# VectorE's instructions moved between slots in a fused linear-attention and feed-forward kernel

## The reference

```
q, k, v = xn Wq', xn Wk', xn Wv'           (512 -> 128 each)
r_t     = q_t M_t',  M_{t+1} = 0.99 M_t + v_t' k_t / 4    (a scan over the 2048 steps)
s       = (r Wo') * sigmoid(gate)           (128 -> 512)
h       = layernorm(xn) * gamma + beta
y       = silu(h W1 + b1)                   (512 -> 2048)
z       = y W2 + b2                         (2048 -> 512)
g       = silu(xn + 0.5 z)
out     = x + s * g
```

## Time and profile before

| | |
|---|---|
| three runs | 1338.12, 1339.03, 1340.52 us; median 1339.03 |
| the profiled execution | 1339.37 us; its span 1337.6 us, mean granted clock 0.977 |
| busy, share of the span | TensorE 92%, VectorE 84%, ScalarE 80%, GpSimd 29% |
| chunk 0 (from 51.7 us) | 97.0 us |
| chunks 1 to 14, each | 77.6 us |
| chunk 15 and the tail slots | 73.5 us and some 28.7 us |

### The profile page before, as it was taken

How to read it: one execution, slowest core, us unless ns; L and a number is a source line. 1 busy time by engine, 2 the same in 40 slices (tenths; PEclk the granted TensorE clock), 3 DMA queues, 4 the chain that set the end, 5 groups by cost and what they waited for, 6 DMA issues and landing times.

```text
span 1337.6 us, 19050 instructions
## 1 busy us (share of the span) xinstructions
PE 1225.3 (92%) x6144; PEld 633.7 (47%) x6144; DVE 1121.2 (84%) x1894; ACT 1075.0 (80%) x1885; POOL 382.0 (29%) x465
## 2 busy tenths in 40 slices
PE   1279999999999999999999999999999999999994
PEld 0034454545545454554545455454545545454551
DVE  5978798888979888897988889798888979888774
ACT  1349888888888888888888888888888888888885
POOL 4115241321414132141413214141422314142111
PEclk8579999999999999999999999999999999999998
DMA  9201021120302112030211203021120303011011
GB/s 327 54 2 32 1 57 40 32 64 2 93 1 64 32 33 64 5 91 0 65 31 33 64 12 84 1 75 21 33 63 15 82 1 82 14 36 29 18 46 32
DMA packets 38837, 61.21 MB, mean 46 GB/s; under 512 B 9553, under 2 KB 9809, under 8 KB 38737
## 3 DMA queue, kind: packets, MB, share of 16 engines
q1 hardware_dynamic: 38448, 59.87, 17.4%
q10 hardware_dynamic: 288, 0.08, 0.0%
HBM read 43.14 MB, written 16.78 MB: 45 GB/s over the span
## 4 chain that ended last, share of the span: by engine, by line
PE 67%; DVE 19%; issue 6%; ACT 6%; POOL 1%; DMA 1%; SPq 0%; DVEq 0%; ACTq 0%; POOLq 0%
PE blk L421 26%; PE blk L438 22%; PE side L382 9%; DVE blk L630 7%; PE side L406 3%; DVE y_lo L641 3%; ACT blk L525 2%; PE side L370 2%; DVE g_lo L610 2%; DVE y_hi L636 2%; ACT y_full L518 2%; PE side L359 1%; DVE g_rows L605 1%; ACT h_full L484 1%; DVE fin L657 1%
## 5 line engine op out<-in xcount | busy, mean ns | idle before, releaser
L630 DVE TENSOR_SCALAR blk<-blk,ratio 128x512 f32<-128x512 f32 x768 | 572.5, 753 | 177.7 <-PE blk L421 172.9
L525 ACT ACTIVATE blk<-blk,ratio 128x512 f32<-128x512 f32 x960 | 625.7, 667 | 73.5 <-PE blk L438 66.6
L421 PE MATMUL blk<-h_hi,q_sb 128*128 128x512 f16 x1024 | 391.7, 383 | 73.2 <-DVE blk L630 35.9
L421 PE MATMUL blk<-h_lo,q_sb 128*128 128x512 f16 x1024 | 390.4, 381 | 0.0
L438 PE MATMUL blk<-y_hi,w_sb 128*128 128x512 f16 x1024 | 388.9, 380 | 0.0
L438 PE MATMUL blk<-y_lo,w_sb 128*128 128x512 f16 x1024 | 388.6, 380 | 0.0
L518 ACT ACTIVATE y_full<-blk,par,last 128x512 f32<-128x512 f32 x256 | 199.3, 779 | 41.3 <-PE blk L421 41.3
L641 DVE SCALAR_TENSOR_TENSOR y_lo<-y_full,up,y_hi 128x512 f16<-128x512 f32 x256 | 228.3, 892 | 0.1
L938 POOL TENSOR_TENSOR out_sb<-fin,s_rows 128x512 f32<-128x512 f32 x62 | 80.2, 1294 | 446.4 <-ACT fin L537 443.1
L421 PEld LDWEIGHTS blk<-h_hi,q_sb 128*128 128x128 f16 x1024 | 100.3, 98 | 218.7 <-DVE blk L630 102.6
L923 POOL TENSOR_TENSOR h_lo<-h_full,h_hi 128x512 f16<-128x512 f32 x64 | 86.8, 1356 | 388.2 <-DVE h_hi L614 373.9
(11 more groups left out here) (132 smaller groups left out, 1151.2 us busy)
## 6 DMA issues: line engine op xcount, KB each, us to landing
xt<-in_x SPq DMA_DIRECT2D x64, 256.0 KB, 4.8
x_again<-in_x SPq DMA_DIRECT2D x256, 64.0 KB, 1.9
out<-out_sb SPq DMA_DIRECT2D x256, 64.0 KB, 1.7
w_sb<-in_q SPq DMA_DIRECT2D x4, 1024.0 KB, 13.8
zt<-in_q SPq DMA_DIRECT2D x2, 1024.0 KB, 15.4
y_hi<-in_q SPq DMA_DIRECT2D x1, 1024.0 KB, 10.1
y_lo<-in_q SPq DMA_DIRECT2D x1, 1024.0 KB, 12.3
s_rows<-in_wqkv SPq DMA_DIRECT2D x1, 768.0 KB, 7.9
```

The source lines that it names most:

```text
L421: mm = pe.matmul(blk[J % 2][:], q1_sb[:, g, j // 4, w, j % 4 * P:(j % 4 + 1) * P], a[:, c % 2, g, :], start=(g == 0 and n == 0), stop=(g = ...
L525: act.activation(blk2[hb][:], blk2[hb][:], ACT.Copy, scale=ratio2[:, KC * j + hb:KC * j + hb + 1]).then_inc(blk2_scaled, 1)
L630: dve.tensor_scalar(blk[J % 2][:], blk[J % 2][:], ratio1[:, at:at + 1], None, ALU.mult).then_inc(blk_scaled, 1)
```

## The change

Only the written-out order changes; the same instructions are issued. `turned_low` is cut in two: g_lo stays two slots after the transposes, the cast h_hi (with its wait for the old h) goes to three (HHIGH_LAG), and h_lo on GpSimd to four (HLOW_LAG). y_low goes to five slots after the last fc1 pair of an even J and three after that of an odd J. Transposes, statistics, moments, rows and normalise get other slots. In ScalarE's and GpSimd's loops nothing is edited, but what hangs on turn, turn_z and ROWS_AT moves along.

```diff
-TURN_AT = (43, 49, 54, 59)
-TURN_Z_AT = (18, 21, 26, 30)
-STATS_AT, MOMENTS_AT, ROWS_AT, NORMALISE_AT = (18, 21, 22, 24), (25, 26), 28, (34, 36, 38, 40)
+TURN_AT = (43, 48, 54, 59)
+TURN_Z_AT = (18, 21, 25, 28)
+STATS_AT, MOMENTS_AT, ROWS_AT, NORMALISE_AT = (16, 17, 20, 24), (25, 27), 30, (33, 34, 37, 40)
 FIN_LAG, OUT_LAG = 2, 3
-TURN_LAG, HLOW_LAG, READ_LAG = 2, 3, 1
+TURN_LAG, HHIGH_LAG, HLOW_LAG, READ_LAG = 2, 3, 4, 1
+
+YHIGH_LAG, YLOW_LAG = 1, (5, 3)
...
                 dve.tensor_tensor(g_lo[:, k, :], bank[:], g_hi[:, k, :], ALU.subtract).then_inc(g_lo_done, 1)
+
+            def h_high(c, k):
+                dve.wait_ge(turn_act, 2 * (4 * c + k + 1))
                 if k == 0 and c >= 2:
...
                 turned_low(0, n - 1, first_turn_bank[n - 1])
+                h_high(0, n - 1)
...
             turned_low(0, 3, first_turn_bank[3])
+            h_high(0, 3)
...
                     turned_low(*side_job(G - TURN_LAG)[1:], side[JOB_BANK[G - TURN_LAG]])
+                if G >= HHIGH_LAG and side_job(G - HHIGH_LAG) and side_job(G - HHIGH_LAG)[0] == "turn":
+                    h_high(*side_job(G - HHIGH_LAG)[1:])
                 if before and before[0] == "read":
                     remember(*before[1:], side[JOB_BANK[G - 1]])
-                if G >= 1 and (at := fc1_step(G - 1)) and at[1] == KC - 1:
+                if G >= YHIGH_LAG and (at := fc1_step(G - YHIGH_LAG)) and at[1] == KC - 1:
                     y_high(at[0])
-                if G >= 2 and (at := fc1_step(G - 2)) and at[1] == KC - 1:
-                    y_low(at[0])
+                for odd in (0, 1):
+                    at = fc1_step(G - YLOW_LAG[odd]) if G >= YLOW_LAG[odd] else None
+                    if at and at[1] == KC - 1 and at[0] % 2 == odd:
+                        y_low(at[0])
```

## The result

Measured: 1352.44 us (median of four runs, 1351.86 to 1353.88) against 1338.72 for the kernel before; ratio 1.0102, 95% interval 1.0084 to 1.0119. The changed kernel is 13.7 us slower; the forecast was 6.4 slower. The profiled execution took 1353.88 us, its span is 1352.1, so 14.5 us more of span than before.

A forecast was written before the change was run, and what follows sets the result against it. TensorE's product stream was taken as the bound. Late rows +2.1 minus 1.5 gained gave +0.55 us for each of chunks 1 to 14 (+7.7), chunk 15 -0.9, tail -0.4, chunk 0 0: +6.4 on 1339.0, 1345.4 us, range 1331 to 1356.

The forecast's parts named there:

- The likeliest case: Whole kernel: late rows cost more than the other parts gain, +0.55 us in each of chunks 1 to 14, 1345.4 us; chance 0.40.
- What bounds it: TensorE's product stream sets the time, busy 75.8 of 77.6 us; reordering VectorE can win at most 3.1 us a chunk.
- part 1: Low halves of y move to slots 3 and 6 (mod 8), without a rescale; nobody waits; gain with h's cast 1.5 us.
- part 2: h's cast one slot later: fewer instructions in slots 45, 56, 61; gain with y's low halves 1.5 us a chunk.
- Part 3, the rows: Row scalars behind tile 2's output on GpSimd: g_rows at slot 33 waits 3 us, delaying slot 36; loss 2.1 us a chunk.
- Moving the statistics from slots 18 to 24 into 16 to 24 ... costs nothing: Statistics in slots 16 to 24: no cost, since rows would have to wait anyway and slots 16 to 20 keep up.
- Chunk 15, forecast -0.9: Last chunk, with no next chunk to prepare: 1.1 us of holes, mostly behind y_lo, so -0.9 us.
- The clock, given a chance of 0.02: Rival: TensorE's hole at slot 36 halves the granted clock, losing 3.4 us a chunk, 1393 us; chance 0.02.
- The forecast of 0 for the rest of chunk 0: Chunk 0: late rows cost some 2.9 us, crowded slots 43 to 59 give some 3 back: 0, from -2 to +2.
- Rows on time: Rival: GpSimd reaches the rows as early as now, all else as forecast; 26.5 us won, 1312 us; chance 0.05.
- Late, but without the small holes: Rival: rows late, but the small walked holes are absent; 7.7 us won, 1331 us; chance 0.15.
- More conflicts: Rival: y_lo of slots 30, 35, 59 and g_rows of 34 meet GpSimd's work; +1.2 us a chunk, 1355; chance 0.26.

The follow-up runs named there:

- The first experiment: Changed kernel with ROWS_AT 27 instead of 30, so the row scalars stand ahead of the output of tile 2 on GpSimd's queue: 1314.15 us, ratio 0.981 to the kernel before.

## Why the prediction came out as it did

**Direction, mechanism and range held; the size was off by a factor of two.** The likeliest case was the one that happened, with a part of the rivals on the clock and on the conflicts. That the range held is partly luck: it left out the clock and had no term for slot 22, and its upper end came from the conflicts, of which only some 0.8 us, in chunk 15, reached the time.

*What bounds it; part 1 and part 2.* Right. The gain between slot 36 and the next slot 0 was 1.61 us a chunk, the walk had 1.5, with its three small holes: 0.24, 0.31 and 0.25 forecast at slots 54, 59 and 64, and 0.22, 0.31 and 0.27 measured. Slot 46 kept its 0.41.

*Part 3, the rows.* Right in every link, each some 0.3 us later in the chunk than forecast, which is the hole of slot 22 below: the output's silu over at 658.68, so 37.4 us into the chunk (forecast 37.1), row_z at 45.96 us (forecast 45.6), wait 2.7 us (forecast 3), and slot 24 to slot 36 took 17.60 us against 15.47 before, +2.13 where the sum has +2.1. The first experiment shows that this one place is worth 2.45 us a chunk.

*The term that failed: "Moving the statistics from slots 18 to 24 into 16 to 24 ... costs nothing".* I had checked that no rescale would be late, and not who else stands behind a statistics step. The step that updates the memory, at slot 21, does, and the wo product of slot 22 takes the side bank that this step frees: 0.26 us a chunk, 3.6 us in all. The row of the wait is the second of the waits above. In the rows, first before, then after, the product of slot 22 stands behind rescale 21 and the memory step, and after the change a statistics step stands ahead of both:

```profile
640.59 0.76 DVE L630 TENSOR_SCALAR blk<-blk,ratio 128x512 f32<-128x512 f32 x1 [0.38 <-PE blk L421]
641.26 0.28 DVE L624 SCALAR_TENSOR_TENSOR mem_t<-mem_t,side 128x128 f32<-128x128 f32 x1
...
642.12 1.02 PE L406 MATMUL side<-wo_sb,r_t 128*128 128x512 f32 x2
...
647.55 0.69 DVE L598 BATCH_NORM_STATS2 stat<-xt 128x6 f32<-128x512 f32 x1
648.15 0.74 DVE L635 TENSOR_SCALAR blk<-blk,ratio 128x512 f32<-128x512 f32 x1
648.80 0.28 DVE L629 SCALAR_TENSOR_TENSOR mem_t<-mem_t,side 128x128 f32<-128x128 f32 x1
...
649.14 1.12 PE L408 MATMUL side<-wo_sb,r_t 128*128 128x512 f32 x2
```

The two experiments with the statistics at 21 show the cause: the wait and the hole are gone from both.

*Chunk 15, forecast -0.9, came out at 0.* Its new hole of 0.83 us at slot 34 lies behind the y_lo of slot 30 and the y_hi of slot 31, which last 1.45 and 1.12 us beside GpSimd's outputs:

```profile
1289.11 1.45 DVE L646 SCALAR_TENSOR_TENSOR y_lo<-y_full,up,y_hi 128x512 f16<-128x512 f32 x1
1290.48 0.75 DVE L635 TENSOR_SCALAR blk<-blk,ratio 128x512 f32<-128x512 f32 x1
1291.14 1.12 DVE L641 TENSOR_SCALAR y_hi<-y_full,up 128x512 f16<-128x512 f32 x1
```

I had named these conflicts as a rival and left them out of this chunk's sum.

*The clock, given a chance of 0.02.* It was in fact part of the outcome. The step that failed is the reading of one row as a rule: a hole of 2.3 us had left the clock up once, in the tail, and I took this for what shorter holes would do. The hole of 2.2 us, no longer than that one, left it up in thirteen of fifteen chunks; the other two (chunks 0 and 13) cost 1.7 us each, half of the 3.4 that the rival had. The forecast of 0 for the rest of chunk 0 fits: without the 1.7 it is 0.1 below the kernel before. But chunk 0 takes 93.3 us in the first experiment and 95.4 in the one that differs from it by one statistics slot, so a fit to 0.1 is partly chance.

*The sum again*: 6.4 forecast, + 3.6 for slot 22, + 0.9 for chunk 15, + 3.4 for the clock, + 0.6 for a later start of the loop (where the order of the instructions is the same; over all the profiles it starts at 51.6 to 52.5 us), and - 0.4 for all roundings and the tail, give the 14.5 us of the two profiled executions. The medians differ by 13.7.

*The rivals.* "Rows on time" was priced at 1312 and measured, as an experiment, at 1314. "Late, but without the small holes" did not happen: they were there to 0.03 us. "More conflicts" happened in chunk 15 and at slots 33 and 34 of the others, where they cost nothing since the rows set the end. So one sign of being right failed: y_lo's mean was to be below 0.89 us and is 0.90, and 59 of 256 take over 1.2 us against 45 before. The new y_lo of slots 30 and 35 meet GpSimd's outputs, as the rival had it.

*Left open.* Why the clock drops after some holes of 2.2 us and not after others was not tried. Nor did the new slots of the transposes get a run of their own: they were changed only together with other parts.

## What to carry to other kernels

When work is moved between slots of written-out queues, list for each moved instruction what stands behind it on its own engine and, for each of these, who waits for it, small steps that free a bank included: here an update of 0.3 us held up a product. A latency chain on a slow engine (5.6 us of tiny steps) belongs ahead of that engine's bulk work, whose results nobody waits for; swapping the two cost more than everything that the rest of the change won. And a part that is good can be hidden by one that is bad: measured alone, the new slots of y's low half were 20 us faster.

## What the runs showed of the hardware that was not expected

A hole of TensorE of 2.2 us was followed by a lower granted clock in 2 of 15 chunks in one profile and in 4 of 15 in another whose queue order differs by one statistics step; a hole of 4.5 us (4.3 idle) in 14 of 14. In chunk 0, where the hole is 2.3 us, the clock fell in all three profiles that have it; in chunks 1 to 14 it fell after 1 and after 3 of 14. Each drop at the shorter hole made slot 36 last 4.5 instead of 2.82 us, and the longer one 4.1 to 5.5.

A hole of 1.7 us (1.55 idle) can do it too. At slot 59 of chunk 0 the kernel before and the kernel with only its rows late have the same hole; the clock stayed up in the first and fell to half in the second. Their rows at that slot, the kernel before first:

```profile
143.63 0.39 PE L421 MATMUL blk<-h_hi,q_sb 128*128 128x512 f16 x1 [1.55 <-DVE blk L630]
140.00:150.00 10.00, 7.93 (x38) 3.44 (x37) 8.66 (x16) 8.49 (x15) 3.91 (x5) 1.00 0.00 0
...
143.52 0.44 PE L421 MATMUL blk<-h_hi,q_sb 128*128 128x512 f16 x1 [1.55 <-DVE blk L630]
143.70:147.00 3.30, 3.30 (x11) 1.75 (x10) 0.43 (x2) 2.31 (x4) 1.44 (x2) 0.50 0.00 0
```

So the length of the hole alone does not decide it in these profiles.

VectorE and GpSimd hold each other up in both directions: y_lo took up to 1.75 us instead of 0.74 (the row at 669.31) when an output step was under way, and GpSimd's first rows step 0.65 instead of 0.20 when y_lo was. Rescales, which read and write PSUM, took 0.72 to 0.76 us in every profile.
